# A rebuilt prologue, first step and tail for a cross-attention and mixture-of-experts kernel on one core

## The reference

```python
xn, ln = layernorm(ctx), layernorm(x)                  # x takes the part of the latents
q = ln @ W_q
k, v = split(concat([xn @ W_kv, ln @ W_kv]))           # 77 + 256 = 333 keys, 4 heads of 64
sim = (rmsnorm(q) / 8) @ rmsnorm(k).T                  # masked context keys get -max
x1 = x + softmax(sim) @ v @ W_out + b_out
h = layernorm(x1)
scores = sigmoid(h @ gate.T)                           # 8 experts, 2 groups, best group, top 2
w = 2.5 * normalized top-2 scores
out = x1 + relu(h @ shared_up.T)**2 @ shared_down.T
      + sum_e w[e] * (relu(h @ up[e].T)**2 @ down[e].T)
```

## Time and profile before

| | us |
|---|---|
| median of 3 runs | 1220.6 (1220.33 to 1220.65) |
| profiled execution, its own time | 1214.58 |
| its span, first to last instruction | 1212.7 |
| busy: TensorE, VectorE, ACT, GpSimd | 1166.7, 1018.3, 783.3, 543.0 |
| a middle step, start to start | 36.20 |
| first matmul of the prologue | 15.88 |
| first K/V product | 20.61 |
| first score product | 33.70 |
| last issue of the store (256 KB) | 1210.15 |

### The profile page before, as it was taken

How to read it: one execution, slowest core, us unless ns; L and a number is a source line. 1 busy time by engine, 2 the same in 40 slices (tenths; PEclk the granted TensorE clock), 3 DMA queues, 4 the chain that set the end, 5 groups by cost and what they waited for, 6 DMA issues and landing times.

```text
span 1212.7 us, 29627 instructions
## 1 busy us (share of the span) xinstructions
PE 1166.7 (96%) x10176; PEld 1095.3 (90%) x10176; DVE 1018.3 (84%) x3529; ACT 783.3 (65%) x1829; POOL 543.0 (45%) x477
## 2 busy tenths in 40 slices
PE   3699999999999999999999999999999999999996
PEld 2499999999999999999999999999999999999996
DVE  3688888898888898888898888898888889888876
ACT  2576666676566676666777666677666677666663
POOL 4144543454443454453444454444454444444432
PEclk9799999999999999999999999999999999999999
DMA  5000000000000000000000000000000000000000
GB/s 166 12 13 22 22 20 3 22 22 22 22 22 2 22 22 22 22 22 2 22 22 22 22 22 7 17 22 22 22 22 10 13 22 22 22 21 11 2 11 18
DMA packets 28228, 25.86 MB, mean 21 GB/s; under 512 B 6640, under 2 KB 27536, under 8 KB 28080
## 3 DMA queue, kind: packets, MB, share of 16 engines
q1 hardware_dynamic: 27744, 23.83, 6.3%
q0 software_dynamic: 336, 0.14, 0.2%
HBM read 15.57 MB, written 8.39 MB: 20 GB/s over the span
## 4 chain that ended last, share of the span: by engine, by line
PE 94%; DVE 2%; ACT 2%; POOL 1%; DMA 1%; issue 1%; POOLq 0%; DVEq 0%; ACTq 0%
PE up_ps L282 11%; PE up_ps L284 10%; PE up_ps L283 10%; PE down_ps L282 9%; PE down_ps L284 7%; PE down_ps L283 7%; PE attn_ps L392 7%; PE attn_ps L378 7%; PE attn_ps L282 4%; PE attn_ps L283 4%; PE attn_ps L284 4%; PE attn_ps L364 3%; PE attn_ps L331 2%; PE attn_ps L366 2%; PE attn_ps L368 2%; PE attn_ps L343 1%
## 5 line engine op out<-in xcount | busy, mean ns | idle before, releaser
L1198 POOL TENSOR_TENSOR hid_lo<-relu,hid_hi 128x512 fp32r<-128x512 f32 x192 | 247.0, 1287 | 272.8 <-DVE hid_hi L1006 161.8
L1021 DVE SCALAR_TENSOR_TENSOR acc<-down_ps,route_w,acc 128x256 f32<-128x256 f32 x512 | 222.1, 476 | 20.8 <-PE down_ps L284 14.8
L282 PE MATMUL down_ps<-down_hi,hid_hi 128*128 128x256 f32 x768 | 230.3, 300 | 4.0 <-POOL hid_lo L1198 2.1
L282 PE MATMUL up_ps<-x_hi,up_hi 128*128 128x256 f32 x768 | 227.9, 297 | 1.5 <-ACT x_hi L667 1.2
L284 PE MATMUL down_ps<-down_hi,hid_lo 128*128 128x256 f32 x768 | 216.3, 282 | 0.0
L283 PE MATMUL down_ps<-down_lo,hid_hi 128*128 128x256 f32 x768 | 215.8, 281 | 0.0
L284 PE MATMUL up_ps<-x_hi,up_lo 128*128 128x256 f32 x768 | 214.4, 279 | 0.0
L283 PE MATMUL up_ps<-x_lo,up_hi 128*128 128x256 f32 x768 | 214.3, 279 | 0.0
L638 ACT ACTIVATE probs<-masked,neg_max,q_scale 128x333 f32<-128x333 f32 x256 | 168.5, 659 | 57.8 <-DVE neg_max L863 57.8
L678 ACT ACTIVATE relu_sb<-up_ps 128x512 f32<-128x512 f32 x192 | 113.5, 591 | 72.0 <-PE up_ps L284 72.0
L282 PEld LDWEIGHTS down_ps<-down_hi,hid_hi 128*128 128x128 f32 x768 | 144.8, 188 | 16.2 <-issue 14.1
(11 more groups left out here) (153 smaller groups left out, 2927.9 us busy)
## 6 DMA issues: line engine op xcount, KB each, us to landing
out<-acc SPq DMA_DIRECT2D x32, 256.0 KB, 2.2
x_first<-in_x SPq DMA_DIRECT2D x16, 256.0 KB, 2.8
w_stage<-in_x SPq DMA_DIRECT2D x16, 256.0 KB, 2.8
up_stage<-in_up_t SPq DMA_DIRECT2D x1, 1536.0 KB, 11.4
down_stage<-in_down_t SPq DMA_DIRECT2D x1, 1536.0 KB, 14.8
c_first<-in_ctx SPq DMA_DIRECT2D x16, 77.0 KB
w_stage<-in_ctx SPq DMA_DIRECT2D x16, 77.0 KB
mask_in<-in_mask SPq DMA_DIRECT2D x32, 9.6 KB, 2.5
```

The lines of the kernel that those rows point to most:

```text
L282: nc.tensor.matmul(out_ap, s_hi, m_hi, start=first, stop=False)
L1021: nc.vector.scalar_tensor_tensor(acc[:, t, :], down_ps[:, (e + 1) % 2, t * D:(t + 1) * D], route_w[:, t, e:e + 1], acc[:, t, :], ALU.mult, ...
L1198: nc.gpsimd.tensor_tensor(hid_lo[:, p % HID_RING, :], relu2[:, p % 2, :], hid_hi[:, p % HID_RING, :], ALU.subtract).then_inc(hid_lo_done, 1)
```

## The change

The middle steps keep their instructions and their order. Changed are:

- **Transfers.** The layer norm vectors and gammas come as one tensor `vec` on SP's queue. SP's order is x, context, `vec`, w_kv, w_q, mask, gate, then a wait for w_kv, up, w_out, row 1, down. GpSimd issues only the output bias and the gate bias, behind its memsets (`rows_in`).
- **Weight splits.** `w_stage` is split in three (K/V, query, output), `up_stage` in four column blocks, all low parts on VectorE; `down_stage` in four row blocks, the low parts on GpSimd in step 0 behind `residual`. ACT makes the high parts of `up_stage` in the prologue. VectorE does up block 0 before the first mask and blocks 1 to 3 between the first and the second four masks.
- **Row 1.** Its statistics and reciprocal root come in the prologue and its normalization before the first mask of step 0.
- **Filler.** `keep_warm(20)` issues 20 transposes of the identity, whose result nobody reads, at three places of TensorE's prologue.
- **Last step.** TensorE does the probabilities times V before expert products 2 to 5, and products 6 and 7 after the last transposes; VectorE's order follows.
- **Closing part.** `up` of pair 3 goes before the shared products, the other ups one place earlier; VectorE adds the shared result before its last three router levels.
- **Store.** The last row is stored in two halves.

The diff, cut to its core:

```diff
+        QUART = 4
+        WARM = 20
+        WQ, WKV, WOUT = slice(0, D), slice(D, 3 * D), slice(3 * D, 4 * D)
+        UP_COLS = [slice(i * F * P // QUART, (i + 1) * F * P // QUART) for i in range(QUART)]
+        DOWN_ROWS = [slice(i * F // QUART, (i + 1) * F // QUART) for i in range(QUART)]
...
                 if b == 1:
-                    sp.wait_ge(w_lo_done, 1)
+                    sp.wait_ge(w_lo_done, 2)
...
+            sp.dma_start(vec[:], vectors).then_inc(vectors_in, DMA)
+            sp.dma_start(w_stage[:, :, WKV], w_kv.rearrange("(k p) n -> p k n", p=P)).then_inc(kv_in, DMA)
+            sp.dma_start(w_stage[:, :, WQ], w_q.rearrange("(k p) n -> p k n", p=P)).then_inc(q_in, DMA)
             load_mask(0)
-            sp.dma_start(w_stage[:, :, 0:D], w_q.rearrange("(k p) n -> p k n", p=P)).then_inc(weights_in, DMA)
-            sp.dma_start(w_stage[:, :, D:3 * D], w_kv.rearrange("(k p) n -> p k n", p=P)).then_inc(weights_in, DMA)
-            sp.dma_start(w_stage[:, :, 3 * D:4 * D], w_out.rearrange("(k p) n -> p k n", p=P)).then_inc(weights_in, DMA)
-            sp.dma_start(gate_stage[:], gate_t.rearrange("(k p) n -> p k n", p=P)).then_inc(weights_in, DMA)
+            sp.dma_start(gate_stage[:], gate_t.rearrange("(k p) n -> p k n", p=P)).then_inc(gate_in, DMA)
+            sp.wait_ge(kv_in, DMA)
             sp.dma_start(up_stage[:], up_t.rearrange("(k p) n -> p k n", p=P)).then_inc(up_in, DMA)
+            sp.dma_start(w_stage[:, :, WOUT], w_out.rearrange("(k p) n -> p k n", p=P)).then_inc(out_in, DMA)
+            load(1)
...
-            store(B - 1)
-            sp.wait_ge(stored, B * DMA)
+            last = out[B - 1].rearrange("(t p) d -> p t d", p=P)
+            for t in range(T):
+                sp.wait_ge(acc_done, (B - 1) * ACC + ACC - T + t + 1)
+                sp.dma_start(last[:, t, :], acc[:, t, :]).then_inc(stored, DMA)
+            sp.wait_ge(stored, (B - 1 + T) * DMA)
...
+            def keep_warm(n):
+                for i in range(n):
+                    nc.tensor.transpose(down_ps[:, 0, 0:P], ident[:], ident[:])
...
+                if not following:
+                    transpose_probs(b, 7)
+                    spread_inverse(b, following)
+                    for pair in range(4):
+                        probs_times_v(b, pair)
+                    ffn("down", 2)
+                    ffn("down", 3)
+                    project_out(b, 0, following)
+                    project_out(b, 1, following)
+                    ffn("down", 4)
+                    ffn("down", 5)
+                    transpose_x2(b)
+                    ffn("down", 6)
+                    ffn("down", 7)
+                    return
...
             pe.wait_ge(consts, 1)
+            keep_warm(WARM)
             transpose_ln(0, False)
+            keep_warm(WARM)
             pe.wait_ge(w_lo_done, 1)
             project_kv(0, 1)
             project_kv(0, 2)
             project_kv(0, 0)
+            pe.wait_ge(w_lo_done, 2)
             project_q(0)
+            keep_warm(WARM)
             steps(step)
             up(B - 1, 0, False, False)
             router(B - 1)
             up(B - 1, 1, False, False)
             up(B - 1, 2, False)
+            up(B - 1, 3, False)
             for t in range(T):
                 down_shared(B - 1, t, False)
-            up(B - 1, 3, False)
+            up(B - 1, 4, False)
             down_expert(B - 1, 0, False)
             down_expert(B - 1, 1, False)
-            up(B - 1, 4, False)
-            down_expert(B - 1, 2, False)
-            down_expert(B - 1, 3, False)
             up(B - 1, 5, False)
-            for e in range(4, E):
+            for e in range(2, E):
                 down_expert(B - 1, e, False)
...
-                    split_hi(2, down_hi[:], down_stage[:])
+                    for rows in DOWN_ROWS:
+                        split_hi(down_hi[:, rows, :], down_stage[:, rows, :])
...
-            act.wait_ge(weights_in, 4 * DMA)
+            act.wait_ge(kv_in, DMA)
+            split_hi(w_hi[:, :, WKV], w_stage[:, :, WKV])
+            act.wait_ge(vectors_in, DMA)
+            ln_full(0, True)
+            act.wait_ge(q_in, DMA)
+            split_hi(w_hi[:, :, WQ], w_stage[:, :, WQ])
+            act.wait_ge(gate_in, DMA)
             nc.scalar.activation(gate_parts[:, :, 0:E], gate_stage[:], ACT.Copy)
-            split_hi(0, w_hi[:], w_stage[:])
-            act.wait_ge(vectors_in, 10 * DMA)
-            ln_full(0, True)
-            for part in range(2):
-                k_squares(0, part, True)
-                v_out(0, part, True)
+            k_squares(0, 0, True)
+            act.wait_ge(out_in, DMA)
+            split_hi(w_hi[:, :, WOUT], w_stage[:, :, WOUT])
+            v_out(0, 0, True)
+            act.wait_ge(up_in, DMA)
+            split_hi(up_hi[:, :, UP_COLS[0]], up_stage[:, :, UP_COLS[0]])
+            k_squares(0, 1, True)
+            v_out(0, 1, True)
             q_out(0, True)
+            for cols in UP_COLS[1:]:
+                split_hi(up_hi[:, :, cols], up_stage[:, :, cols])
...
+            def up_parts(*parts):
+                for i in parts:
+                    dve.wait_ge(w_hi_done, 4 + i)
+                    split_lo(up_lo[:, :, UP_COLS[i]], up_stage[:, :, UP_COLS[i]], up_hi[:, :, UP_COLS[i]])
...
-                    dve.wait_ge(w_hi_done, 2)
-                    split_lo(up_lo[:], up_stage[:], up_hi[:])
-                    dve.wait_ge(w_hi_done, 3)
-                    split_lo(down_lo[:], down_stage[:], down_hi[:])
-                if following:
+                    normalize1(1, False)
+                    up_parts(0)
+                if following and not first:
                     layer_norm1(b + 1, False)
                 mask_scores(b, 0, first)
                 mask_scores(b, 1, first)
                 mask_scores(b, 2, first)
                 mask_scores(b, 3, first)
                 negate_max(b, 0)
+                if first:
+                    up_parts(1, 2, 3)
...
+                if not following:
+                    high(5)
+                    attn_out(b, first)
+                    attn_low(b, 0)
+                    attn_low(b, 1)
+                    add(2)
+                    add(3)
+                    residual_half(b, 0)
+                    residual_half(b, 1)
+                    layer_norm2(b, first)
+                    add(4)
+                    normalize2(b, first)
+                    add(5)
+                    x2_low(b)
+                    add(6)
+                    add(7)
+                    return
...
             layer_norm1(0, True)
+            normalize1(0, True)
+            dve.wait_ge(vectors_in, DMA)
+            nc.vector.tensor_tensor(gam_qk[:], gam_q, gam_k, ALU.mult).then_inc(gamma_done, 1)
+            dve.wait_ge(w_hi_done, 1)
+            split_lo(w_lo[:, :, WKV], w_stage[:, :, WKV], w_hi[:, :, WKV])
+            ln_high(0, True)
+            dve.wait_ge(w_hi_done, 2)
+            split_lo(w_lo[:, :, WQ], w_stage[:, :, WQ], w_hi[:, :, WQ])
+            dve.wait_ge(zeroed, 3)
             mask_keys(0)
-            dve.wait_ge(vectors_in, 10 * DMA)
-            nc.vector.tensor_tensor(gam_qk[:], gam_q[:], gam_k[:], ALU.mult).then_inc(gamma_done, 1)
-            normalize1(0, True)
-            dve.wait_ge(w_hi_done, 1)
+            k_norms(0, 0, True)
+            dve.wait_ge(w_hi_done, 3)
             nc.vector.tensor_tensor(gate_parts[:, :, E:2 * E], gate_stage[:], gate_parts[:, :, 0:E], ALU.subtract)
-            split_lo(w_lo[:], w_stage[:], w_hi[:])
-            ln_high(0, True)
-            k_norms(0, 0, True)
+            split_lo(w_lo[:, :, WOUT], w_stage[:, :, WOUT], w_hi[:, :, WOUT])
             k_norms(0, 1, True)
+            layer_norm1(1, False)
             k_normalize(0, 0, True)
             k_normalize(0, 1, True)
             q_low(0)
             q_norms(0, True)
             dve.wait_ge(gamma_done, 1)
+            dve.wait_ge(rows_in, 2 * DMA)
...
-            route(f, *range(10))
-            route(f, *range(10, 19))
+            route(f, 0)
+            route(f, *range(1, 10))
+            route(f, *range(10, 16))
             add_shared(f, False)
             hidden_high(f, 3, False)
+            route(f, *range(16, 19))
             add_expert(f, 0)
+            hidden_high(f, 4, False)
             add_expert(f, 1)
-            hidden_high(f, 4, False)
             add_expert(f, 2)
-            add_expert(f, 3)
             hidden_high(f, 5, False)
-            for e in range(4, E):
+            for e in range(3, E):
...
+                if first:
+                    for i, rows in enumerate(DOWN_ROWS):
+                        pool.wait_ge(w_hi_done, 4 + QUART + i)
+                        nc.gpsimd.tensor_tensor(down_lo[:, rows, :], down_stage[:, rows, :], down_hi[:, rows, :],
+                                                ALU.subtract).then_inc(down_lo_done, 1)
...
             nc.gpsimd.memset(minus_half[:], -0.5)
```

(24 more changed lines are left out.)

59 lines of the change are left out of this document (24 added, 35 removed).

## The result

| | median us | runs | ratio to before, 95% interval |
|---|---|---|---|
| before | 1220.46 | 4 (1217.22 to 1220.65) | |
| after | 1198.08 | 4 (1197.70 to 1199.18) | 0.9824 [0.9807, 0.9842] |

The change makes the kernel 1.8% faster, 22.4 us between the medians. The profiled execution after took 1197.93 us with a span of 1196.1, so between the two profiled executions only 16.6 us went. Both differences need explaining: 16.6 against 13.7, and 22.4 against 16.6.

The account below looks back on a forecast made before the run. TensorE was taken to fill the middle steps, leaving only the two ends to gain. 9.2 + 1.5 + 2.7 + 0.3 = 13.7 us, from 1220.6 to 1206.9 us; range 1200.5 to 1212.

Parts of the forecast that it names:

- part 3: Step 0, to the fifth softmax: GpSimd's and VectorE's split pieces take turns; softmax at 38.3 against 47.54, 9.2 us earlier.
- the middle steps: Thirty steps with TensorE busy 36.20 of 36.20 us, order of instructions unchanged: they can give nothing.
- Parts 1 and 2: Head: first K/V product at 12.3 against 20.61, full rate through filler; first score product at 23.4, 10.3 us earlier.
- Part 4: Last step, reordered: the final feed-forward starts 1.5 us earlier (bounds 0.5 and 2.5).
- The last sign it gave: End of the kernel: the final feed-forward takes some 25.2 us instead of 28.24.
- Parts 5 and 6: Final feed-forward: smaller waits give 2.7 us (bounds 1.5 and 3.5); store in halves gives 0.3 us (0 to 0.5).
- rival D: Middle steps stretch by 0.45 us a step, so nothing reaches the end: 1220.6 us, chance 0.03.
- I let that stand: Whole kernel: the median of the runs stays 6.0 us above the profiled execution, as before the change.
- A: Step 0: turns don't alternate, VectorE runs its three pieces together, up to 5.6 us more gain: 1201.3 us, chance 0.17.
- B: Late w_kv, cold filler, tail at lower bounds: up to 6.6 us less, half taken; 1210.4 to 1213.5 us, chance 0.17.
- C: Step 0: GpSimd's down pieces far slower than 1.85 us; at 6 us a piece 1223.5 us, chance 0.03.
- The low clock in step 0 that the forecast feared: Step 0: a low clock after TensorE's new idle time, named among the likeliest ways to be wrong; no size.

Follow-up runs that it names:

- no_filler: The changed kernel without its 60 filler transposes: 1201.00 us, ratio 0.9853.
- down_later: The changed kernel with GpSimd's four down pieces waiting for the second negated maximum of step 0: 1193.95 us, ratio 0.9804.
- last_filler: The changed kernel with 16 filler transposes in the last step, while TensorE waits for the last transposes: 1196.58 us, ratio 0.9826.
- null_before: The kernel before, unchanged, timed and profiled once more: 1218.52 us, ratio 0.9998.
- before_packed: The kernel before with its four small vectors held in one tensor, no instruction changed: 1215.63 us, ratio 0.9986.
- pad_after_vec: The changed kernel with 64 unused bytes per partition between the vectors and the later tensors in SBUF: 1199.83 us.

## Why the forecast missed, step by step

**What bounds the kernel, and the shape of the answer:** right. Middle steps stayed full, the gain came from both ends, and the positions on the way lie within 0.3 us of the forecast up to the first score.

**The account.** Between the profiled executions 16.6 us went where 13.7 were forecast: part 3 gave 2.2 us more, the middle steps 2.2 us that were put at nothing, the last step 1.5 us less. The other 5.8 us lie between the profiled executions and the medians, where the forecast let a constant stand.

**Parts 1 and 2:** right in mechanism and size (12.24 for 12.3; 23.72 for 23.4). no_filler confirms that the filler is free and what it buys, 2.4 us in the traces and 2.9 in the medians. The Trainium skill (TensorE: Matmul & The Clock Gate, Part 1) has activity release a slow default, and the two runs agree: 0.42 us between products without it, 0.23 with.

**Part 3: a count was wrong.** The engines do take turns; down_later, where they don't meet, has each of VectorE's three pieces at 0.9 us (2.69 in all). But the sum put four GpSimd pieces of 1.85 us on the chain, and the second did not stand where I put it, before up piece 1. The negated maximum waited out GpSimd's first piece (27.15 to 28.34). Up piece 1, next in VectorE's queue, began at 28.26, and GpSimd's second piece at 28.27 (a row can begin before the one ahead of it on its engine has ended). Up piece 1 took 0.94 us, as it does alone, and GpSimd's piece 2.61, so VectorE went first and GpSimd waited. Then came piece 2, up 2, piece 3, up 3, and the fourth GpSimd piece ran beside the masks from 34.10. That is three pieces on the chain, not four: 1.85 us of the 2.2 us between 38.3 and 36.12. The small rest is 0.25 us less in each of the two turns (2.5 us of both, not 2.75) and 0.15 in the masks, against 0.35 by which up piece 1 ended later than one piece less would give. The group by tile in after:
```profile
L1280 POOL TENSOR_TENSOR down_lo<-down_stage,down_hi x4: 1824/2519/2610, 26.5 to 33.3; 128x768 fp32r<-128x768 f32 x4
```
Its columns are the least, median and greatest ns. The forecast's 1.85 us is near the least, 1.82, the piece that waited for nobody; the others hold 0.7 to 0.8 us of VectorE's work. The Trainium skill (SBUF — State Buffer, "SBUF: two separate sides") has whoever starts first keep the shared ports for the whole instruction, for a VectorE instruction with two inputs in SBUF against a GpSimd one that reads SBUF; the trace agrees, with VectorE's 0.16 us instruction at 1.19 and its 0.9 us pieces at up to 2.6.

**Part 4: right at the full clock, lost to the clock.** Its 1.5 us are measured: 1.6 at the last transposes in after itself, and 33.51 to 31.94 for the step with the clock held (last_filler). In after itself the bunched products left TensorE with one idle time of 2.37 us, the clock fell for 3.4 us, and the stretch came out at 33.48, with nothing gained against the first trace. The forecast named a low clock only for the head. The last sign it gave, a final feed-forward of 25.2 us from the last transposes on, came out at 26.9 in after and at 25.4 in last_filler.

**Parts 5 and 6:** right, 2.9 us for 3.0. From the closing part's logits to the end of VectorE's last add it is 21.4 us before and 18.9 after, 2.6 for part 5's 2.7; from there to the end of the span 2.6 and 2.2, 0.4 for part 6's 0.3. The terms inside part 5's sum were not tested one by one.

**The middle steps: 0 was wrong.** They gave 2.2 us, from where the tensors lie in SBUF: the pad takes it away and the packing alone gives it. The forecast looked at windows rounded to 36.20 and at the order of the instructions, and rightly found both unchanged. That 0.07 us a step adds up over thirty was not in it, and rival D had only the other sign. What in the address matters is not settled.

**"I let that stand" was wrong, and it is the largest error.** I took the 6.0 us between the old median and the old profiled execution as a constant that the new kernel would keep. About half of it was the cost of a clock that falls in the old tail, which that one execution had been spared: null_before's tail is 3.3 us longer, filler there gives 3.0 us in the timed runs, and the old kernel's fastest runs are those with the highest clock. After's median (1198.08) lies on its profiled execution (1197.93), so nothing like it came back. That the new closing part is spared because it has less idle time is likely, and not shown. Of the 5.8 us between the two differences (22.4 and 16.6), about 3 are shown by this. Another 2 lie between the median of before in the first four runs, 1220.46, and the 51 later ones, 1218.2 to 1218.5; whether they are a difference of chips or of so few runs stays open.

**The rivals.** A's time (1201.3) is nearer than the forecast's, but its mechanism did not happen: of the three GpSimd pieces that it takes off the chain one fell away, and the turns still cost some 4 us. B, C and D did not happen either: w_kv landed in time (7.10), GpSimd's first piece took 1.82 us, the middle steps got shorter. The low clock in step 0 that the forecast feared did come (26.0 to 39.6), but the old kernel has one there too (31.3 to 48.4), and the fifth softmax was not late. In B, half of 6.6 us is 3.3, not 3.5; nothing hangs on it.

## What to carry to other kernels

A gap between the profiled execution and the median is itself a reading: ask which stretch differs between executions, and whether the change removes it, before it is added to a forecast. Before weights are split between VectorE and GpSimd at the same time, look whether one of the two can wait: here a single wait on the engine that nobody was late for gave some 4 us. Where a thin tail leaves TensorE idle, filler products in the wait can hold the clock at no cost in the order (1.5 us in the trace of one tail, 3.0 us in the runs of the other), but filler in one place does not decide where the clock falls next.

## What the runs showed of the hardware

- The place of tensors in SBUF changes TensorE-bound steps: 36.10 to 36.12 us a step against 36.17 to 36.20 with the same instructions (before_packed, pad_after_vec), 0.2% of the kernel.
- The granted clock fell for 3.4 us in after's tail, behind one idle time of 2.37 us, and for 10.2 us in null_before's, behind idle times of 1.39, 1.75 and 1.15 us. With the same three idle times it stayed full in another execution of that kernel. The old kernel's runs spread over 6.1 us (1214.7 to 1220.8), the slower ones at the lower mean clock.
- VectorE's next instruction in its queue went ahead of a GpSimd instruction that came up 0.01 us later (28.26 and 28.27), although VectorE had been served just before. From there on the turns alternated, 2.5 us for one of both.
